# Clamping seven experts' weights to ternary values on GpSimd instead of VectorE, in a fused block of attention and quantised experts

## The chip, the cores and the metric

The kernel runs on one core of one Trainium2 chip. The metric is device microseconds for one execution, lower is better. The core has five engines that run their own instruction streams and wait for each other by semaphores: TensorE (PE in the profile), VectorE (DVE), ScalarE (ACT), GpSimd (POOL) and SyncE (SP), which here only issues loads and stores.

## The reference, cut to what matters

Four layers follow one another on `x` of 16 x 64 x 256 values: a cross attention with 32 heads of width 8, a mixture of eight experts with ternary weights, a latent cross attention, and a mixture of 32 masked experts. The change touches the weights of the second layer:

```python
def weight_quant(w):
    scale = 1.0 / jnp.maximum(jnp.mean(jnp.abs(w)), EPS)
    return jnp.clip(jnp.round(w * scale), -1.0, 1.0) / scale

def expert_ffn(x, gw, uw, dw):          # for each of the 8 experts
    gate = bitlinear(x, gw)
    up = bitlinear(x, uw)
    activated = up * jnp.square(jax.nn.relu(gate))
    return bitlinear(activated, dw)
```

Each of the 24 matrices (gate, up and down of eight experts) is divided by its own mean magnitude, rounded, and clipped to -1, 0 or 1.

## The kernel before, in words

The 1024 tokens are eight tiles of 128 rows. The first layer goes tile by tile, and the weights of one expert are quantised beside each tile, so that tile `t` and expert `t` share one turn of the loops on TensorE, ScalarE and VectorE. Nothing orders the work but the program order of each engine and its semaphores.

One turn of the first layer runs so. TensorE makes the scores of a tile (`natural`, L650) and VectorE takes the row maxima of each head straight from four PSUM banks (`maxima`, L1426). VectorE splits the maxima into three bfloat16 parts (`split_max`, L1433 to L1436), TensorE turns them (L660), VectorE copies them out (`unturn_max`, L1442), and TensorE subtracts them from the scores (`less_max`, L674). ScalarE takes the exponentials (L1166), TensorE turns the probabilities (L683), ScalarE copies them out (L1172), TensorE weighs the values (`weigh`, L698), ScalarE copies the result (L1188), TensorE turns it back (L705), and VectorE divides and adds to `X` (`add_att`, L1447 to L1451). The scores of tile `t + 1` (L650) wait for all four exponentials of tile `t`.

The weights pass through four hands. SyncE loads expert `e` into one of three buffers `raw` (it waits for `raw_used`). ScalarE sums the magnitudes of the three matrices (`magnitudes`, L1180, which uses `W` as a place to write to), TensorE adds over the rows (L667), and VectorE takes mean and reciprocal (`mean`, L1456 to L1458). VectorE then scales the three matrices, takes the minimum with 1 and rounds them to 16-bit whole numbers that lie in the place of the bfloat16 weights (`over_mean`, L1461, three instructions of 128 x 1024 values, the last of which adds one to `raw_used`). Last, one instruction of 128 x 3072 values clamps these whole numbers to -1..1 and writes bfloat16 into the same place (`ternary_of`, L1464).

The order on VectorE in turn `t` is: `mean(t)`, `over_mean(t, 0)`, the maxima of tile `t + 1` and their split, `add_att(t - 1)`, `over_mean` of the two other matrices, a wait for `raw_used` (VectorE's own count), `ternary_of(t)`, `queries(t + 3)` (L1421, the normalised rows `qn`, up to turn 4), and `statistics` (L1398). Turn 6 also centres the router's weights (`r_raw`, L1504 to L1506).

GpSimd has little to do in this layer. It builds constants, waits for the context and the tables, and rotates the keys of the third layer: four `tensor_tensor` on 128 x 1024 or 128 x 512 values for `kvr2` and four of half that size for `kvr` (L559 to L562, each waiting for the one before), one copy (L563), and three instructions on 23 columns (L564 to L566). It then waits for `roots_ready`, which VectorE gives at the end of the layer, and normalises four tiles of `XN` (L568, L570). TensorE needs the rotated keys after the router's logits (L721, L767).

At the end of the layer TensorE weighs the values of the last tile (L698, after VectorE's `att` of the tile before, L1448), turns the result, and computes the router's logits (L721) and the turned keys (L767). ScalarE copies them out, and VectorE picks the two best experts of each token (L458, L461). The first matmul with the ternary weights comes after that.

Of the kernel before, what the change touches and what calls it, by code (L numbers as in the profile page):

```python
# [7 lines left out]
F32, F32R, BF16, I16, I32, U32 = mybir.dt.float32, mybir.dt.float32r, mybir.dt.bfloat16, mybir.dt.int16, mybir.dt.int32, mybir.dt.uint32  # L8
ALU, ACT, AX = mybir.AluOpType, mybir.ActivationFunctionType, mybir.AxisListType
P = 128  # L10
NT = 8
# [9 lines left out]
NE = 8  # L21
# [75 lines left out]
def build(nc, x, ctx_in, cst_in, sel_in, kv_in, router_w, ffn_w, fold_in,  # L97
          weight_t, scale, masks_t, router_dt, out):
    with ExitStack() as ctx:
# [3 lines left out]
        def sb(name, shape, dt=F32):  # L103
            n = int(np.prod(shape[1:])) * (2 if dt == BF16 else 4)
            at = place[0]
            place[0] = (at + n + 31) // 32 * 32
            places[name] = at
            return nc.alloc_sbuf_tensor_at(name, shape, dt, offset=at)
# [5 lines left out]
        def sem(name):  # L114
            return ctx.enter_context(nc.semaphore(name))
# [38 lines left out]
        W = sb("W", [P, NE, 3, 4 * H], BF16)  # L154
# [179 lines left out]
        raw_used, w_summed, w_total, w_rec_ready, hid_acted = (sem(n) for n in ("raw_used", "w_summed", "w_total", "w_rec_ready", "hid_acted"))  # L334
# [204 lines left out]
        def _(pool):  # L539
# [9 lines left out]
            link(pool.memset(before[:], 0.0))  # L549
            pool.affine_select(out=before[:], in_=before[:], compare_op=ALU.is_ge, fill=1.0, base=0,  # L550
                               pattern=[[-1, P]], channel_multiplier=1).then_inc(bconsts_built, 1)
            pool.wait_ge(ctx_loaded, 16)
            pool.wait_ge(cst_loaded, 16)
            for dst, src in ((kvr2[:], ctx2), (kvr[:, :, 0, :], ctxn)):
                n = src.shape[1]
                r = rot[:, 0:n, :]
                cos = cst[:, None, C_KCOS:C_KCOS + S].to_broadcast([P, n, S])
                sin = cst[:, None, C_KSIN:C_KSIN + S].to_broadcast([P, n, S])
                link(pool.tensor_tensor(dst, src, cos, ALU.mult))  # L559
                link(pool.tensor_tensor(r[:, :, 0:32], src[:, :, 32:64], sin[:, :, 0:32], ALU.mult))  # L560
                link(pool.tensor_tensor(r[:, :, 32:64], src[:, :, 0:32], sin[:, :, 32:64], ALU.mult))
                link(pool.tensor_tensor(dst, dst, r, ALU.add))  # L562
            pool.tensor_copy(kvr[:, :, 1, :], kvr[:, :, 0, :]).then_inc(kv_rotated, 1)  # L563
            link(pool.tensor_scalar(spare[:], cst[:, C_IOTA:C_IOTA + NBLK], float(P), float(2 * NT * P), ALU.mult, ALU.add))  # L564
            link(pool.tensor_scalar(slot_of[:, 0, :], spare[:], -1.0, None, ALU.mult))
            pool.tensor_scalar(slot_of[:, 1, :], spare[:], -1.0, float(NT * P), ALU.mult, ALU.add).then_inc(bconsts_built, 1)  # L566
            pool.wait_ge(roots_ready, 1)
            link(pool.tensor_scalar(less_mean[:], mv[:, :, 0], -1.0, 0.0, ALU.mult, ALU.add))  # L568
            for t in range(NT // 2, NT):
# [820 lines left out]
        def _(dve):  # L1390
# [5 lines left out]
            def statistics(tiles):  # L1396
                for t in tiles:
                    ins = dve.bn_stats(stats[:, t, :], X[:, t, :])  # L1398
                link(ins)
# [18 lines left out]
            def queries(t):  # L1418
                if t >= 2:
                    dve.wait_ge(q_turned, t - 1)  # L1420
                dve.tensor_scalar(qn[t % 2][:], X[:, t, :], mv[:, t, 0:1], rstd_q[:, t:t + 1], ALU.subtract,  # L1421
                                  ALU.mult).then_inc(qn_ready, 1)

            def maxima(t, kvl):
                dve.wait_ge(nat_ready, 4 * t + kvl + 1)
                dve.tensor_reduce(mx[:, kvl, :], bank[kvl][:].rearrange("p (h s) -> p h s", s=S), AX.X, ALU.max).then_inc(nat_read, 1)  # L1426

            def split_max(t):
                dve.wait_ge(nat_read, 4 * t + 4)
                if t:  # L1430
                    dve.wait_ge(mx_turned, t)
                m = mx[:].rearrange("p a h -> p (a h)")
                link(dve.tensor_copy(mx_parts[:, 0, :], m))  # L1433
                link(dve.tensor_tensor(mx_rest[:], m, mx_parts[:, 0, :], ALU.subtract))
                link(dve.tensor_copy(mx_parts[:, 1, :], mx_rest[:]))
                dve.tensor_tensor(mx_parts[:, 2, :], mx_rest[:], mx_parts[:, 1, :], ALU.subtract).then_inc(mx_ready, 1)  # L1436

            def unturn_max(t):
                dve.wait_ge(mx_turned, t + 1)
                if t >= 2:  # L1440
                    dve.wait_ge(scores_ready, 4 * t - 4)
                dve.tensor_copy(mxT[t % 2][:], bank[7].bitcast(BF16)[0:96, 4 * P:5 * P]).then_inc(mxT_ready, 1)  # L1442

            def add_att(t):
                dve.wait_ge(o_turned, t + 1)
                o = bank[6][:].rearrange("p (n a) -> p n a", a=32)[:, :, 0:2 * (HD + 1)].rearrange("p n (g e) -> p n g e", g=2)
                link(dve.reciprocal(den_rec[:], o[:, :, :, HD]))  # L1447
                dve.tensor_tensor(att[:].rearrange("p (n g d) -> p n g d", g=2, d=HD), o[:, :, :, 0:HD],  # L1448
                                  den_rec[:, :, :, None].to_broadcast([P, NPAIR, 2, HD]), ALU.mult).then_inc(att_read, 1)
                dve.wait_ge(att_read, t + 1)  # L1450
                dve.tensor_tensor(X[:, t, :], X[:, t, :], att[:], ALU.add).then_inc(x1_ready, 1)  # L1451

            def mean(e):

                dve.wait_ge(w_total, e + 1)
                link(dve.tensor_scalar(w_sum2[:], bank[7][:, 3 * P:3 * P + 3], 1.0 / (FF * H), EPS, ALU.mult, ALU.max))  # L1456
                dve.tensor_copy(w_mean[:, e, :], w_sum2[:])
                dve.reciprocal(w_rec[e % 2][:], w_sum2[:]).then_inc(w_rec_ready, 1)  # L1458

            def over_mean(e, m):  # L1460
                return dve.tensor_scalar(W[:, e, m, :].bitcast(I16), raw[e % 3][:, m, :], w_rec[e % 2][:, m:m + 1], 1.0, ALU.mult, ALU.min)  # L1461

            def ternary_of(e):
                dve.tensor_scalar(W[:, e], W[:, e].bitcast(I16), 1.0, -1.0, ALU.min, ALU.max)  # L1464
# [17 lines left out]
            for t in range(NT):  # L1482
                mean(t)
                dve.wait_ge(w_rec_ready, t + 1)
                over_mean(t, 0)
                if t + 1 < NT:
                    for kvl in range(4):
                        maxima(t + 1, kvl)
                    split_max(t + 1)
                    unturn_max(t + 1)  # L1490
                if t:
                    add_att(t - 1)
                over_mean(t, 1)
                over_mean(t, 2).then_inc(raw_used, 1)
                dve.wait_ge(raw_used, t + 1)
                ternary_of(t)
                if t + 3 < NT:
                    queries(t + 3)
                if t:
                    dve.wait_ge(x1_ready, t)  # L1500
                    statistics([t - 1])
                if t == NT - 2:
                    dve.wait_ge(r_loaded, 16)
                    link(dve.bn_stats(r_stats[:], r_raw[:]))  # L1504
                    link(dve.bn_aggr(r_mv[:], r_stats[:]))
                    dve.tensor_scalar(r_raw[:], r_raw[:], r_mv[:, 0:1], None, ALU.subtract).then_inc(r_centred, 1)  # L1506
# [275 lines left out]
            n = 8 * NGROUP  # L1782
# [162 lines left out]
```

## Time and profile before

| | us |
|---|---|
| median of 3 runs | 478.03 |
| lowest and highest | 476.23 and 480.19 |
| the profiled execution's own time | 480.91 |
| its span in the trace | 479.0 |
| VectorE busy in the span | 347.0 (72%) |
| GpSimd busy in the span | 137.9 (29%) |
| ScalarE busy in the span | 213.7 (45%) |

A span is the time from the first to the last instruction of the profiled execution. In the rows below the first number of a timeline's row is the start in us from the span's start and the second the duration in us; what stands in square brackets is how long the engine was idle before, and what released it. In the chain of waits the rows are the pieces that ended last, in order of time.

### The profile page before, as it was taken

The numbers are of one execution on the slowest core, as the hardware profiler recorded it, in microseconds if no ns is written. First come the engines' busy times: TensorE is split into PE (matmuls) and PEld (weight loads), VectorE is DVE, ScalarE is ACT, GpSimd is POOL, SyncE is SP. The second block draws the span as 40 slices with busy tenths as digits, with TensorE's granted clock in tenths as the row PEclk, the third lists the DMA queues.
The fourth block names the chain that finished last, engine by engine and source line by source line (L and its number), as shares of the span: only waits on it lengthen the run. The fifth ranks groups of instructions, "written<-read, shape, count | busy, mean of one in ns | idle before, by whom it ended". The sixth has DMA issues, their size and how long they took to land.

```text
span 479.0 us, 10598 instructions
## 1 busy us (share of the span) xinstructions
PE 379.1 (79%) x3676; PEld 259.6 (54%) x3677; DVE 347.0 (72%) x876; ACT 213.7 (45%) x474; POOL 137.9 (29%) x147
## 2 busy tenths in 40 slices
PE   2566867771687778797989999999999989548991
PEld 1344545671244444575555664664655878436881
DVE  4998898979788989386686876977868525663551
ACT  1578787825278778479010231221211321224440
POOL 1064000020667774300031421412403410161332
PEclk9989798955589999899999999999999999859997
DMA  8975562041144661171021120220220201341010
GB/s 299 423 300 189 191 219 104 10 168 46 39 132 152 196 200 57 46 263 36 1 90 47 42 90 9 82 89 2 89 89 1 89 1 54 124 130 58 25 35 22
DMA packets 16895, 50.77 MB, mean 106 GB/s; under 512 B 2072, under 2 KB 6304, under 8 KB 14800
## 3 DMA queue, kind: packets, MB, share of 16 engines
q1 hardware_dynamic: 13984, 42.46, 24.6%
q0 software_dynamic: 2864, 7.68, 5.3%
q8 instruction: 30, 0.49, 0.4%
q14 instruction: 17, 0.14, 0.1%
HBM read 43.44 MB, written 6.69 MB: 105 GB/s over the span
## 4 chain that ended last, share of the span: by engine, by line
PE 61%; DVE 14%; ACT 10%; issue 8%; POOL 5%; DMA 1%; ACTq 0%; DVEq 0%; POOLq 0%
PE bank L941 15%; PE bank L1147 7%; PE bank L953 6%; PE bank L1024 6%; PE bank L964 3%; PE bank L837 3%; PE bank L650 2%; PE bank L1000 2%; PE bank L977 2%; DVE mx L1426 2%; PE bank L803 2%; POOL y_rows L589 2%; ACT pnat L1166 2%; ACT W L1180 2%; POOL xg L582 1%
## 5 line engine op out<-in xcount | busy, mean ns | idle before, releaser
L1637 DVE TENSOR_TENSOR roped<-bank,cst 128x512 f32<-128x512 f32 x96 | 61.8, 686 | 30.2 <-PE bank L941 28.6
L596 POOL TENSOR_TENSOR WE<-WE,wT 128x512 f32<-128x512 f32 x32 | 40.5, 1299 | 140.9 <-DMA WE<-_L_ffn_expert_masks_dram 140.9
L1307 ACT ACTIVATE qrT<-bank 128x512 f32<-128x512 f32 x16 | 8.7, 596 | 82.2 <-PE bank L964 82.2
L941 PE MATMUL bank<-XNT_hi,AW_hi 128*128 128x512 f32 x96 | 41.3, 430 | 2.3 <-DVE roped L1637 1.6
L941 PE MATMUL bank<-XNT_hi,AW_lo 128*128 128x512 f32 x96 | 37.8, 394 | 0.0
L941 PE MATMUL bank<-XNT_lo,AW_hi 128*128 128x512 f32 x96 | 37.8, 393 | 0.0
L953 PE MATMUL bank<-roped,MW 128*64 128x512 f32 x128 | 31.0, 605 | 0.0
L1024 PE MATMUL bank<-VW,ctxT 128*128 128x256 f32 x128 | 30.8, 386 | 0.0
L941 PEld LDWEIGHTS bank<-XNT_hi,AW_hi 128*128 128x128 f32 x96 | 18.0, 187 | 22.0 <-DVE roped L1637 12.1
L582 POOL DMA_INDIRECT xg<-x_rows,owner_b x23 | 22.8, 993 | 24.0 <-DVE owner_b L420 14.8
L803 PE MATMUL bank<-W,xgT 128*128 x92 | 27.1, 422 | 2.2 <-ACT xgT L1243 2.2
L589 POOL DMA_INDIRECT y_rows<-y,slot x23 | 22.7, 986 | 17.8 <-ACT y L1261 14.4
L1172 ACT ACTIVATE pT<-bank 128x512 f32<-128x512 f32 x32 | 19.3, 604 | 15.9 <-PE bank L683 15.9
L1180 ACT ACTIVATE W<-raw 128x1024 bf16<-128x1024 f32 x24 | 25.4, 1061 | 0.0
L1024 PEld LDWEIGHTS bank<-VW,ctxT 128*128 128x128 f32 x128 | 23.2, 190 | 3.5 <-issue 0.8
L814 PE MATMUL bank<-identf,hid 128*128 128x128 f32 x92 | 15.5, 292 | 11.7 <-ACT hid L1265 6.9
L1426 DVE TENSOR_REDUCE mx<-bank 128x8 f32<-128x512 f32 x32 | 19.8, 681 | 5.1 <-PE bank L650 5.1
L1147 PE MATMUL bank<-WE,pT_d 128*128 x80 | 21.5, 409 | 1.5 <-ACT pT_d L1385 1.3
L1255 ACT ACTIVATE hidT<-bank,less_magic 128x512 bf16<-128x512 f32 x23 | 15.8, 687 | 12.3 <-PE bank L814 11.6
L683 PE MATMUL bank<-identf,pnat 128*128 128x128 f32 x128 | 20.8, 298 | 0.0
L941 PEld LDWEIGHTS bank<-XNT_hi,AW_lo 128*128 128x128 f32 x96 | 18.0, 188 | 4.3
L1301 ACT ACTIVATE prob<-prob 128x512 f32<-128x512 f32 x16 | 10.1, 632 | 22.3 <-DVE prob L1647 22.3
(297 smaller groups left out, 893.9 us busy)
## 6 DMA issues: line engine op xcount, KB each, us to landing
raw<-in_L_ffn_w_dram SPq DMA_DIRECT2D x8, 1536.0 KB, 6.4
fold<-in_L_xattn_fold_dram SPq DMA_DIRECT2D x8, 1024.0 KB, 5.2
WE<-_L_ffn_expert_masks_dram SPq DMA_DIRECT2D x8, 1024.0 KB, 5.4
kv<-in_keys_values_dram SPq DMA_DIRECT2D x8, 656.0 KB, 7.6
yg<-y_rows SPq DMA_DIRECT2D x8, 256.0 KB, 4.7
x_tok<-pay SPq DMA_DIRECT2D x8, 256.0 KB, 2.3
X<-in_x_dram SPq DMA_DIRECT2D x4, 256.0 KB, 9.3
ctx_sb<-in_ctx_dram SPq DMA_DIRECT2D x1, 768.0 KB, 18.4
```

The costliest lines, as they stand in the source:

```text
L582: pool.indirect_dma_start(out=xg[j % 4][:].bitcast(U32), out_offset=None, in_=x_rows, in_offset=bass.IndirectOffsetOnAxis(ap=RB.owner[:, j ...
L589: pool.indirect_dma_start(out=y_rows, out_offset=bass.IndirectOffsetOnAxis(ap=slot[:, b:b + 1], axis=0), in_=y[b % 4][:], in_offset=None). ...
L596: pool.tensor_tensor(WE[:, e], WE[:, e], wT[:], ALU.mult).then_inc(WE_ready, 1)
L683: mm = pe.transpose(bank[4 + kvl % 2][:, c * P:(c + 1) * P], pnat[kvl][:, c * P:(c + 1) * P], identf[:])
L803: mm = pe.matmul(bank[2 + 2 * m - par][:], xgT[par][:, k * P:(k + 1) * P], W[:, bass.ds(e, 1), m, k * FF:(k + 1) * FF].rearrange("p a i -> ...
L941: mm = pe.matmul(bank[g][:], a[:, k, c * P:(c + 1) * P], b[:, k, g * 512:(g + 1) * 512], start=k == 0 and i == 0, stop=k == 1 and i == 2)
L953: pe.matmul(bank[2 + g][half(h, g) * S:(half(h, g) + 1) * S, :], MW[u][:, r, at:at + S], roped[n][:, r, :], start=r == 0, stop=False, skip ...
L1024: mm = pe.matmul(bank[t % 4][:, 0:H], ctxT[:, u, t * P:(t + 1) * P], VW[:, u, :], start=u == 0, stop=u == NU - 1)
L1147: mm = pe.matmul(bank[4 + r % 4][:, 0:H], pT_d[r % 4][:, k * P:(k + 1) * P], WE_k[:, bass.ds(e, 1), k, :].rearrange("p a o -> p (a o)"), s ...
L1180: ins = act.activation(W[:, e, m, :], raw[e % 3][:, m, :], ACT.Abs, accum_out=w_sum[e % 2][:, m:m + 1])
L1426: dve.tensor_reduce(mx[:, kvl, :], bank[kvl][:].rearrange("p (h s) -> p h s", s=S), AX.X, ALU.max).then_inc(nat_read, 1)
L1637: ins = dve.tensor_tensor(roped[n][:, r, :].rearrange("p (b s) -> p b s", s=S), src, cst[:, None, at:at + S].to_broadcast([P, 8, S]), ALU. ...
```

## The change

GpSimd runs `ternary_of` for experts 0 to 6, between and behind its instructions for the rotation, each after a wait for the expert's `raw_used`. VectorE keeps only expert 7. The instruction is the same in shape, operations and place.

```diff
@@ GpSimd @@
+            def ternary_of(e):
+                pool.wait_ge(raw_used, e + 1)
+                pool.tensor_scalar(W[:, e], W[:, e].bitcast(I16), 1.0, -1.0, ALU.min, ALU.max)
+
+            ternary_of(0)
             pool.wait_ge(ctx_loaded, 16)
             pool.wait_ge(cst_loaded, 16)
             for dst, src in ((kvr2[:], ctx2), (kvr[:, :, 0, :], ctxn)):
...
                 link(pool.tensor_tensor(dst, dst, r, ALU.add))
+                ternary_of(1 if n == 2 * NT else 2)
             pool.tensor_copy(kvr[:, :, 1, :], kvr[:, :, 0, :]).then_inc(kv_rotated, 1)
...
+            for e in range(3, NE - 1):
+                ternary_of(e)
             pool.wait_ge(roots_ready, 1)
@@ VectorE @@
                 over_mean(t, 2).then_inc(raw_used, 1)
                 dve.wait_ge(raw_used, t + 1)
-                ternary_of(t)
+                if t == NT - 1:
+                    ternary_of(t)
                 if t + 3 < NT:
                     queries(t + 3)
```

## Rows read from the trace of the kernel before

**Rows 1.** Busy us (and instructions) of PE, PEld, DVE, ACT and POOL, by stretch

```profile
14.00:46.00 32.00, 20.76 (x303) 14.67 (x303) 29.74 (x76) 22.06 (x44) 13.63 (x12) 0.95 0.74 292
46.00:94.00 48.00, 35.86 (x605) 26.96 (x605) 42.71 (x107) 38.24 (x79) 0.00 (x0) 0.89 0.39 142
```

**Rows 2.** The chain of waits, from 32 to 72 us

```profile
32.26 2.48 DVE mx L1426 x4
...
43.42 2.49 DVE mx L1426 x4
...
65.93 1.04 ACT W L1180 x2
```

**Rows 3.** VectorE in order of time: clamps, and maxima that waited for TensorE

```profile
26.61 0.96 DVE L1464 TENSOR_SCALAR W<-W 128x3072 bf16<-128x3072 int16 x1
...
53.72 2.48 DVE L1426 TENSOR_REDUCE mx<-bank 128x8 f32<-128x512 f32 x4 [0.86 <-PE bank L650]
...
60.20 0.96 DVE L1464 TENSOR_SCALAR W<-W 128x3072 bf16<-128x3072 int16 x1
...
69.48 0.96 DVE L1464 TENSOR_SCALAR W<-W 128x3072 bf16<-128x3072 int16 x1
...
82.09 2.48 DVE L1426 TENSOR_REDUCE mx<-bank 128x8 f32<-128x512 f32 x4 [0.77 <-PE bank L650]
...
88.57 0.96 DVE L1464 TENSOR_SCALAR W<-W 128x3072 bf16<-128x3072 int16 x1
```

**Rows 4.** VectorE in order of time: around the clamp of expert 3

```profile
59.42 0.75 DVE L1461 TENSOR_SCALAR W<-raw,w_rec 128x1024 int16<-128x1024 f32 x1
...
61.08 0.41 DVE L1421 TENSOR_SCALAR qn<-X,mv,rstd_q 128x256 f32<-128x256 f32 x1
...
62.33 0.75 DVE L1461 TENSOR_SCALAR W<-raw,w_rec 128x1024 int16<-128x1024 f32 x1
63.00 2.48 DVE L1426 TENSOR_REDUCE mx<-bank 128x8 f32<-128x512 f32 x4
...
66.71 0.22 DVE L1442 COPY mxT<-bank 96x128 bf16<-96x128 bf16 x1 [0.35 <-PE bank L660]
```

**Rows 5.** VectorE and GpSimd in order of time, during the rotation

```profile
27.17 2.27 POOL L559 TENSOR_TENSOR kvr<-ctx_sb,cst 128x1024 f32<-128x1024 f32 x1 [24.24 <-DMA ctx_sb<-in_ctx_dram]
27.48 2.10 DVE L1421 TENSOR_SCALAR qn<-X,mv,rstd_q 128x256 f32<-128x256 f32 x1
29.51 1.10 POOL L560 TENSOR_TENSOR rot<-ctx_sb,cst 128x512 f32<-128x512 f32 x1
29.69 0.96 DVE L1457 COPY w_mean<-w_sum 128x3 f32<-128x3 f32 x1
30.70 1.09 POOL L561 TENSOR_TENSOR rot<-ctx_sb,cst 128x512 f32<-128x512 f32 x1
30.75 1.58 DVE L1461 TENSOR_SCALAR W<-raw,w_rec 128x1024 int16<-128x1024 f32 x1
```

**Rows 6.** GpSimd: groups by line, shapes apart (busy us, mean ns)

```profile
L577 POOL TENSOR_SCALAR hid<-hid,hs 128x512 f32<-128x512 f32 x12 | 8.4, 700 | 0.5
...
L600 POOL MEMSET acc<- 128x2048 f32 x1 | 1.8, 1807 | 0.1
...
L568 POOL TENSOR_SCALAR less_mean<-mv 128x8 f32<-128x8 f32 x1 | 0.2, 203 | 60.4 <-DVEq L1512 60.4
```

**Rows 7.** VectorE and GpSimd in order of time: both on `XN`

```profile
103.12 0.57 POOL L570 TENSOR_SCALAR XN<-X,less_mean,rstd 128x256 f32<-128x256 f32 x1
...
103.19 0.64 DVE L1514 TENSOR_SCALAR XN<-X,mv,rstd 128x256 f32<-128x256 f32 x1
```

**Rows 8.** The end of the layer: VectorE and TensorE in order of time

```profile
90.56 0.34 DVE L1506 TENSOR_SCALAR r_raw<-r_raw,r_mv 8x256 f32<-8x256 f32 x1
...
92.33 0.42 DVE L1448 TENSOR_TENSOR att<-bank,den_rec 128x256 f32<-128x256 f32 x1
...
95.00 0.64 PE L698 MATMUL bank<-pT,kv 128*18 128x64 f32 x32 [0.33 <-ACT pT L1172]
```

## The prediction

> **What bounds the kernel now.** I read the busy times by stretch first, to see how full VectorE and GpSimd are where the clamp runs. From 14 to 46 us VectorE is busy for 29.74 of 32 us, and from 46 to 94 us for 42.71 of 48, while GpSimd works for 13.63 us in the first stretch and not at all in the second [rows 1]. So GpSimd has the time. The chain of waits, read second, says what the clamp is worth. In its pieces from about 15 to 47 us nearly everything is VectorE (the maxima at 32.26 and 43.42 us belong to it), but from there to 95 us it is a loop of ScalarE and TensorE, with ScalarE's sums of the weights in it (65.93 us) [rows 2]. A turn of that loop is 69.48 - 60.20 = 9.28 us [rows 3]. VectorE's own turn is hardly shorter: the wait of 0.35 us for the turned maxima is its only one in such a turn [rows 4], so it works for about 8.9 us. Taking work from VectorE can therefore pay in the first two turns only, and putting more than some 0.4 us of stall on it makes it the bound again, up to what the next engine can wait.
>
> Third I read VectorE and GpSimd side by side, because GpSimd is to run while VectorE goes on. During the rotation some VectorE instructions stretch to the end of the GpSimd instruction beside them. `qn`, 0.41 us elsewhere [rows 4], starts at 27.48 and ends at 29.58, behind a GpSimd instruction that ends at 29.44; the copy of three columns takes 0.96 us and ends at 30.65, with GpSimd's instruction at 30.61; a scaling that takes 0.75 us elsewhere ends at 32.33, 0.54 us after GpSimd's at 31.79 [rows 5]. So these forms (copy and `tensor_scalar` from SBUF to SBUF) stand still while GpSimd runs. GpSimd's `tensor_scalar` does this as well as its `tensor_tensor`: VectorE's `XN` at 103.19 us takes 0.64 us and ends 0.14 after GpSimd's at 103.69 [rows 7]. The maxima, read from PSUM, kept their 2.48 us beside GpSimd (32.26 us) [rows 2].
>
> **The change part by part.** *Removed:* seven clamps of 0.96 us on VectorE; the next instruction starts 0.88 us after each (60.20 to 61.08) [rows 3, 4].
>
> *Added:* seven clamps on GpSimd of length D. The trace has no GpSimd instruction of 3072 values or on 16-bit whole numbers, so D is bounded by its neighbours [rows 6]. `tensor_scalar` takes 0.203 us for 8 columns and 0.700 us for 512: a line through both gives 0.986 ns a column and D = 0.203 + 3064 x 0.000986 = 3.2 us. Six times the 512-column time gives 4.2 us, an upper end. From below, the largest memset needs 1.807/2048 = 0.88 ns a column, 2.7 us, and if more of the 0.700 us is a fixed cost than 0.2, D comes down: a line through the 0.57 us for 256 columns of `XN` [rows 7] and the 0.700 us gives 2.0 us. I take 3.2 us, because its two rows are the same operation with little beside them, and keep 2.2 (2.0 runs faster than the memset writes) and 4.2.
>
> The Trainium skill (GPSIMD Engine Reference, Engine selection) sends elementwise work to VectorE and calls GpSimd roughly line-rate with one input; an estimate from its 1.2 GHz and the 0.2 us start is 2.8 us, by which the sum below would be about +4.5 us. The same page (Elementwise — side-by-side cycle accounting) gives 1.8 cycles an element for a tight loop, an estimate of 4.6 us and about +17 us; the trace's 0.700 us for 512 columns lies between the two.
>
> *The new wait.* GpSimd is released by `raw_used`, at the moment VectorE used to start the clamp; call that S. VectorE goes on to `qn` (S to S + 0.4). VectorE's clamp used to start 0.03 us after the scaling that it waits for (59.42 + 0.75 to 60.20) [rows 3, 4], and no row shows GpSimd quicker than that, so I let `qn` through first. The clamp then runs from S + 0.4 to S + 3.6. The copy of the three means stands behind it, ends 0.04 us later, and the scaling of the next expert's first matrix starts 0.10 us after that, at S + 3.74. The maxima follow 0.67 us later, as at 62.33 to 63.00, at S + 4.41. They came at S + 2.80 (63.00 - 60.20). So a full turn loses 1.61 us, and its length is 9.28 + 1.61 = 10.9 us. Behind the late maxima wait TensorE's subtraction, ScalarE's exponentials, and all of the loop; their slack of about 1.3 us (ScalarE starts an exponential that much after the scores could be ready) holds one such stall, not a repeated one, since VectorE is then busy or blocked all the time.
>
> The turns one by one, delay of S in brackets:
> - Turn 0: after the clamp GpSimd starts the rotation's first instruction (2.27 us [rows 5]), which catches the scaling: 3.67 + 2.27 + 0.54 - 0.07 = 6.41 us after S to the maxima, 5.65 before (32.26 - 26.61), +0.76. The rotation, itself 3.1 us later, then holds the first cast of the maxima's split some 0.9 us more, but is over before three later instructions that it stretched in the old order (a second cast, the addition to `X`, a scaling: 0.33 + 0.39 + 0.35 us). [+0.65 at S1]
> - Turn 1: the second rotation's first instruction, 1.09 us, does the same: 3.67 + 1.09 + 0.54 - 0.07 = 5.23, 2.80 before, +2.4. [+3.05]
> - Turn 2: the copy for `kvr` (a 512-column instruction, 0.7 us) catches the scaling and adds 0.4; of the 1.61 the 0.86 us that the maxima waited for TensorE anyway come off [rows 3]: +1.1. [+4.15]
> - Turns 3 and 4: +1.6 each. [+7.35]
> - Turn 5: there is no `qn`, before or after; 1.61 less the wait of 0.77 us for TensorE [rows 3], +0.8. [+8.15]
> - Turn 6: GpSimd starts at S + 0.1. The centring of the router's weights (8 rows) is of the form that stands still; it ends 0.14 after the clamp, at S + 3.44, where it ended at 90.90 - 88.57 = 2.33 [rows 3, 8], +1.1. [+9.25]
>
> At the end VectorE's `att`, due at 92.75, comes at 102.0. TensorE's weighing of the last tile, 1.1 us, waits for it and ends at 103.1; it ended at 95.64, held by ScalarE's copy [rows 8]. So 1.8 us of the delay vanish there and +7.5 us remain; VectorE's own way to the router's choice, where it kept the clamp of expert 7, is +8.1 us with 0.8 us of idle in front of its join. GpSimd has ended its last clamp several us before `roots_ready`, so `XN` is not later for it, and the loads, which wait for `raw_used`, move with the turns. Everything behind the layer moves by the same +7.5 us.
>
> The sum: 480.91 + 7.5 = 488.4 us against the profiled execution. That execution was 2.9 us above the median of the runs, so I put the same difference on the median: 478.0 + 7.5 = 485.5 us. Each us of D counts seven times.
>
> **The rivals.**
> - *D is short, about 2.2 us.* For: 256 columns take nearly as long as 512 [rows 6, 7]. Against: the memset's rate [rows 6]. A turn of 7.65 + D = 9.85 us is still a little over 9.28, and 7.5 - 7 x 1.0 = +0.5: 478.5 us.
> - *GpSimd is slow on this form, 4.2 us.* 7.5 + 7 x 1.0 = +14.5: 492.5 us. For: whole numbers in and bfloat16 out, which no row shows. Against: in-place form and few operations.
> - *GpSimd gets ahead of `qn`.* Then `qn`, the statistics and the sums come behind the clamp instead of beside it: the maxima at S + 0.1 + D + 1.75, 0.64 us later in each of five turns, +3.2: 488.7 us. For: both are released by the same instruction. Against: VectorE's 0.03 us above.
> - *Not slower: the clamp doesn't hold VectorE back (a 16-bit form that blocks nothing, or runs in under about 1.6 us).* Place: the copy of the three means after each clamp. It decides at 7.65 + D = 9.28, D = 1.63 us, below which ScalarE's loop is the bound again. The gain is then the two clamps on VectorE's stretch of the chain, 2 x 0.88 = 1.8 us: 476.2 us. The other five gain nothing, for the loop there is ScalarE's and TensorE's. Against: [rows 7], a GpSimd `tensor_scalar` that did hold VectorE. The Trainium skill (SBUF — State Buffer, Who interferes with whom) says too that whoever issues first has the shared ports for the whole instruction.
>
> **How the numbers follow.** The forecast (D about 2.8 to 3.7 us) 0.46; slow clamp 0.13; GpSimd ahead of `qn` 0.10; short clamp 0.22; not slower 0.09. About 1% (4.8 us) is what a measurement of this kernel tells from no change. Slower by over 1% takes D over 2.8 us: most of the first three cases, 0.67. Within 1%: the short clamp, most of the last, a little of the first, 0.29. Faster by over 1%, -4.8 us, would need most of 7 x 0.88 = 6.2 us on the path, which the chain speaks against: 0.04. The range runs from the short clamp's side, 477.5, to a slow clamp, 493.5; the forecast's own, for D from 2.8 to 3.7, is 482.5 to 489.
>
> **What would show it right or wrong.** Right: GpSimd's seven clamps of about 3.2 us, one a turn; on VectorE the copy of the three means at about 2.7 us instead of 0.17 in turns 3 to 5; turns of about 10.9 us between the `qn`; the pieces of the chain in the first layer VectorE's and GpSimd's in place of ScalarE's; the second layer's start some 7.5 us later, and from there on the same length. Wrong in size: clamps of another length, with the same picture. Wrong in kind: means of 0.17 us beside a running clamp (no block), turns of 9.3 us in spite of blocked means (more slack than I count), or a `qn` of 3 us (the other order).

## The result: slower by 1.3%, and the profile after

The changed kernel takes 488.23 us (median of 6 runs, 482.00 to 489.81) against 478.45 us before (6 runs, 476.12 to 480.19). The ratio is 1.0134, 95% interval 1.0085 to 1.0182, which on 478.45 us is +6.4 us (+4.1 to +8.7). A second set of six runs gave 1.0142 (1.0087 to 1.0197). Executions of one kernel differ by several us with the clock that TensorE is granted; the ratio compares like with like and the bare medians don't, so 9.8 us between the medians is not the price of the change.

The profiled execution has its own time at 489.74 us and a span of 487.8 us, 8.8 us more than before. The page's parts 1, 4 and 5 (busy time; the shares of the chain of work that ended last, in which DVE had 14% and ACT 10% before; and the new group):

```profile
PE 382.1 (78%) x3670; PEld 263.5 (54%) x3677; DVE 354.9 (73%) x869; ACT 215.5 (44%) x474; POOL 156.6 (32%) x154
...
PE 59%; DVE 20%; issue 9%; ACT 5%; POOL 5%; DMA 1%; DVEq 0%; ACTq 0%; POOLq 0%
...
L554 POOL TENSOR_SCALAR W<-W 128x3072 bf16<-128x3072 int16 x7 | 19.5, 2788 | 61.2 <-DVE W L1469 61.2
```

One line is the point of the case: VectorE is busy for 354.9 us, 7.9 us more than before, although seven clamps of 0.96 us left it. Work went away and busy time grew, so instructions that stayed got longer; in a profile, an instruction that stands still counts as busy. The clamp on GpSimd takes 2.79 us on average.

VectorE in order of time, in turn 1 (the first five rows), in turn 3 (from 60.57 us) and at the start of turn 4's `qn`. It answers to [rows 4]; L1421 is now L1429, L1461 is L1469, L1426 is L1434, L1457 is L1465:

```profile
40.48 0.41 DVE L1429 TENSOR_SCALAR qn<-X,mv,rstd_q 128x256 f32<-128x256 f32 x1
40.81 0.42 DVE L1406 BATCH_NORM_STATS2 stats<-X 128x6 f32<-128x256 f32 x1
41.26 0.16 DVE L1464 TENSOR_SCALAR w_sum<-bank 128x3 f32<-128x3 f32 x1
41.46 2.06 DVE L1465 COPY w_mean<-w_sum 128x3 f32<-128x3 f32 x1
...
45.03 2.47 DVE L1434 TENSOR_REDUCE mx<-bank 128x8 f32<-128x512 f32 x4
...
60.57 1.41 DVE L1469 TENSOR_SCALAR W<-raw,w_rec 128x1024 int16<-128x1024 f32 x2
62.01 2.94 DVE L1429 TENSOR_SCALAR qn<-X,mv,rstd_q 128x256 f32<-128x256 f32 x1
...
65.52 0.17 DVE L1465 COPY w_mean<-w_sum 128x3 f32<-128x3 f32 x1
...
66.47 2.48 DVE L1434 TENSOR_REDUCE mx<-bank 128x8 f32<-128x512 f32 x4
...
72.95 2.94 DVE L1429 TENSOR_SCALAR qn<-X,mv,rstd_q 128x256 f32<-128x256 f32 x1
```

GpSimd in the same turns:

```profile
40.60 2.89 POOL L554 TENSOR_SCALAR W<-W 128x3072 bf16<-128x3072 int16 x1 [3.95 <-DVE W L1469]
...
62.06 2.75 POOL L554 TENSOR_SCALAR W<-W 128x3072 bf16<-128x3072 int16 x1 [5.63 <-DVE W L1469]
73.00 2.75 POOL L554 TENSOR_SCALAR W<-W 128x3072 bf16<-128x3072 int16 x1 [8.19 <-DVE W L1469]
```

Read the ends together. In turn 1 the copy of three columns (0.17 us before) ends at 43.52, 0.03 us after the clamp. The two instructions before it run in the middle of the clamp and are not held: the statistics, which read `X` in SBUF (0.42 us), and a `tensor_scalar` that reads its sums from PSUM (0.16 us), as long as in the kernel before. In turn 3 it is `qn` (0.41 us elsewhere) that ends at 64.95, 0.14 us after the clamp. Between the two `qn` of turns 3 and 4 lie 72.95 - 62.01 = 10.94 us, where a turn took 9.28 [rows 3]. The chain of waits says the same. From 57 to 87 us, where before it was ScalarE's and TensorE's loop [rows 2], it is now VectorE's (a few of its pieces; "issue" is here the stretch inside the blocked `qn`):

```profile
60.57 1.42 DVE W L1469 x2
62.05 2.83 issue
64.88 0.42 DVE stats L1406
...
66.47 2.49 DVE mx L1434 x4
...
71.50 1.42 DVE W L1469 x2
72.98 2.83 issue
...
84.54 2.16 DVE w_mean L1465
```

How the delay grows: S, the start of what follows the last scaling on VectorE, came before at 26.61, 40.62, 49.98, 60.20, 69.48, 78.76, 88.57 us and the last clamp at 94.58. After, the same places are 26.72, 40.48, 51.50, 62.01, 72.95, 83.88, 94.04 and 100.66. The delay is +0.1, -0.1, +1.5, +1.8, +3.5, +5.1, +5.5, +6.1. The router's choice (L458) starts at 113.62 us instead of 107.70, +5.9.

The other 2.9 us of the 8.8 lie behind the layer, in code that nobody touched. More than half of it is in one place: eight matmuls of the last layer (L1024 before, L1032 after) that took 1.97 us at a granted clock of 1.00 take 3.63 us at 0.53. Whether the change did that is a question for the second trace of the kernel before, below.

### The profile page after: what moved, and what is told of

The parts are those of the page before. It is cut to its first block, busy times and chain, and to the rows that moved or that the text cites. A ratio compares the mean times of both kernels' runs of the same rounds, so it can differ in the third digit from the quotient of the medians.

```text
span 487.8 us, 10601 instructions
## 1 busy us (share of the span) xinstructions
PE 382.1 (78%) x3670; PEld 263.5 (54%) x3677; DVE 354.9 (73%) x869; ACT 215.5 (44%) x474; POOL 156.6 (32%) x154
## 4 chain that ended last, share of the span: by engine, by line
PE 59%; DVE 20%; issue 9%; ACT 5%; POOL 5%; DMA 1%; DVEq 0%; ACTq 0%; POOLq 0%
PE bank L949 14%; PE bank L1155 7%; PE bank L1032 6%; PE bank L961 6%; DVE mx L1434 4%; PE bank L972 3%; PE bank L845 3%; PE bank L1008 2%; PE bank L985 2%; POOL y_rows L597 2%; PE bank L811 2%; DVE w_mean L1465 2%; DVE W L1469 2%; POOL xg L590 1%; PE bank L874 1%
## 5 line engine op out<-in xcount | busy, mean ns | idle before, releaser
L554 POOL TENSOR_SCALAR W<-W 128x3072 bf16<-128x3072 int16 x7 | 19.5, 2788 | 61.2 <-DVE W L1469 61.2
L1032 PE MATMUL bank<-VW,ctxT 128*128 128x256 f32 x128 | 32.5, 401 | 0.0
L811 PE MATMUL bank<-W,xgT 128*128 x86 | 25.6, 423 | 2.9 <-ACT xgT L1251 2.6
L1032 PEld LDWEIGHTS bank<-VW,ctxT 128*128 128x128 f32 x128 | 24.2, 198 | 3.8 <-issue 0.8
L1434 DVE TENSOR_REDUCE mx<-bank 128x8 f32<-128x512 f32 x32 | 19.8, 681 | 3.5 <-PE bank L658 3.5
```

Of the source, the lines that this page charges most:

```text
L811: mm = pe.matmul(bank[2 + 2 * m - par][:], xgT[par][:, k * P:(k + 1) * P], W[:, bass.ds(e, 1), m, k * FF:(k + 1) * FF].rearrange("p a i -> ...
L1032: mm = pe.matmul(bank[t % 4][:, 0:H], ctxT[:, u, t * P:(t + 1) * P], VW[:, u, :], start=u == 0, stop=u == NU - 1)
```

## The experiments

The theory: GpSimd's clamp holds VectorE's copy and `tensor_scalar` instructions still for as long as it runs, and seven such holds make the loss. The rivals: the lost time is the order of GpSimd and `qn`; the wait or the hand-over of `W` costs it, not the hold; or the clamps on VectorE were worth more than I thought, in either direction. The start of the router's choice is quoted for each trace as the end of the first layer.

**1. The same clamps at a harmless moment (`window`).** The clamp of expert e starts only when VectorE has scaled the first matrix of the next expert, so that it runs beside the maxima, which are read from PSUM.

```diff
                 pool.wait_ge(raw_used, e + 1)
+                pool.wait_ge(first_scaled, e + 2)
                 pool.tensor_scalar(W[:, e], W[:, e].bitcast(I16), 1.0, -1.0, ALU.min, ALU.max)
...
-                over_mean(t, 0)
+                over_mean(t, 0).then_inc(first_scaled, 1)
```

> GpSimd keeps its seven clamps, but each also waits until VectorE has scaled the first matrix of the next expert, so that it runs beside the maxima, which VectorE reads from PSUM. If the loss is VectorE standing still behind a running clamp (copy and tensor_scalar forms only), the 2.75 us of a clamp fall on 2.48 us of maxima and little is left: turns of about 9.3 us again, 476 to 479 us, at or just under before. If the loss is anything else in having the clamp on GpSimd (later weights, a busy GpSimd, the order of its queue), it stays near 485 us or above, since each clamp now comes later.

Measured: 480.41 us, ratio to the kernel before 1.0004 (0.9962 to 1.0045); the router's choice at 106.25 us. VectorE and GpSimd in turn 3:

```profile
60.20 0.41 DVE L1430 TENSOR_SCALAR qn<-X,mv,rstd_q 128x256 f32<-128x256 f32 x1
...
61.18 0.17 DVE L1466 COPY w_mean<-w_sum 128x3 f32<-128x3 f32 x1
...
62.37 2.75 POOL L555 TENSOR_SCALAR W<-W 128x3072 bf16<-128x3072 int16 x1 [4.70 <-DVE W L1470]
62.54 2.48 DVE L1435 TENSOR_REDUCE mx<-bank 128x8 f32<-128x512 f32 x4 [0.33 <-PE bank L659]
```

The clamp is as long as in the changed kernel and runs on the same engine, with one wait more. It covers the maxima (62.54 to 65.02) and they keep their 2.48 us; the copy has its 0.17 us back. The whole loss is gone (the ratio allows 0.5% either way). So it was neither GpSimd's speed as such nor the hand-over, but what VectorE had to do at that moment.

**2. The clamp in three pieces (`split`).** VectorE can slip in between pieces.

```diff
-                pool.tensor_scalar(W[:, e], W[:, e].bitcast(I16), 1.0, -1.0, ALU.min, ALU.max)
+                for m in range(3):
+                    pool.tensor_scalar(W[:, e, m], W[:, e, m].bitcast(I16), 1.0, -1.0, ALU.min, ALU.max)
```

> Each clamp on GpSimd is cut into three instructions of 128x1024, at the same place. If GpSimd holds VectorE back for one instruction at a time, an instruction of VectorE waits for the rest of one piece of about 1 us, not for 2.75 us: qn, the copy of the means and the scaling go in between, and a turn loses 0 to 0.3 us in place of 1.6: 478 to 480 us. If what counts is GpSimd's total time beside VectorE, it stays at 485 us.

Measured: 481.58 us, ratio 1.0054 (1.0021 to 1.0087), above the 478 to 480 us that I expected; the router's choice at 109.43 us. VectorE and GpSimd in turn 3:

```profile
61.08 1.23 DVE L1430 TENSOR_SCALAR qn<-X,mv,rstd_q 128x256 f32<-128x256 f32 x1
61.12 3.08 POOL L555 TENSOR_SCALAR W<-W 128x1024 bf16<-128x1024 int16 x3 [4.04 <-DVE W L1470]
...
62.87 0.35 DVE L1466 COPY w_mean<-w_sum 128x3 f32<-128x3 f32 x1
...
63.33 1.42 DVE L1470 TENSOR_SCALAR W<-raw,w_rec 128x1024 int16<-128x1024 f32 x1
```

The three pieces take longer together than the one (3.08 us against 2.75), and yet more than half of the loss is gone: `qn` waits 0.82 us for the first piece, the copy 0.18 for the second, the scaling 0.67 for the third, 1.67 us in all where the changed kernel's `qn` alone lost 2.53. VectorE gets its turn at each end of a GpSimd instruction. The hold is per instruction, and its price is at most what is left of that instruction. What I had too low is the loss in a turn: the `qn` of turns 3 and 4 lie 71.31 - 61.08 = 10.23 us apart, about 0.95 more than before and not 0 to 0.3, since three instructions of such a turn wait.

**3. `qn` always first (`qn_first`).** The clamps of experts 0 to 4 also wait until `qn` is done, which takes the rival order away.

```diff
                 pool.wait_ge(raw_used, e + 1)
+                if e + 3 < NE:
+                    pool.wait_ge(qn_ready, e + 4)
```

> The clamps of experts 0 to 4 on GpSimd also wait for VectorE's qn of that turn, so that qn always comes first. If it costs something that GpSimd got ahead of qn in turns 0, 3 and 4, these turns get 0.5 to 0.6 us shorter each and the time falls by 1.5 to 2 us against the changed kernel: about 483 us. If the order doesn't matter, because the copy of the means stands behind the clamp in any case, it stays at 485 us.

Measured: 487.34 us, ratio 1.0158 (1.0114 to 1.0201); the router's choice at 114.13 us, no earlier than in the changed kernel. In turn 3 `qn` has its 0.41 us again, and the copy takes over the stall:

```profile
63.14 0.41 DVE L1431 TENSOR_SCALAR qn<-X,mv,rstd_q 128x256 f32<-128x256 f32 x1
...
63.71 2.75 POOL L556 TENSOR_SCALAR W<-W 128x3072 bf16<-128x3072 int16 x1 [6.15 <-DVE qn L1431]
...
64.12 2.36 DVE L1467 COPY w_mean<-w_sum 128x3 f32<-128x3 f32 x1
...
67.25 2.48 DVE L1436 TENSOR_REDUCE mx<-bank 128x8 f32<-128x512 f32 x4
```

From the start of `qn` to the maxima it is 67.25 - 63.14 = 4.11 us here, against 4.46 (66.47 - 62.01) in the changed kernel, where GpSimd was first: 0.35 us better in turns 3 and 4. But a clamp that waits for `qn` starts 0.57 us behind its start (63.71), where without that wait it began 0.12 us behind it (40.60, turn 1). So turns 1 and 2, in which `qn` had been first already, lose about as much as turns 3 and 4 gain. This way of forcing the order is worth nothing; what the order itself is worth can be read from `scratch`, in the next experiment.

**4. The hold without the hand-over (`scratch`), and no clamps at all (`no_clamp`).** In `no_clamp` VectorE clamps only expert 7; experts 0 to 6 get their scaled weights as bfloat16, neither rounded nor limited from below. In `scratch` GpSimd in addition runs seven clamps of the same form at the same moments, on a tile that nobody reads; the weights are as in `no_clamp`.

```diff
@@ both, VectorE @@
-                return dve.tensor_scalar(W[:, e, m, :].bitcast(I16), raw...
+                into = W[:, e, m, :].bitcast(I16) if e == NE - 1 else W[:, e, m, :]
+                return dve.tensor_scalar(into, raw...
...
-                ternary_of(t)
+                if t == NT - 1:
+                    ternary_of(t)
@@ scratch, GpSimd @@
+            def ternary_of(e):
+                pool.wait_ge(raw_used, e + 1)
+                link(pool.tensor_scalar(scratch[:], scratch[:].bitcast(I16), 1.0, -1.0, ALU.min, ALU.max))
```

> Nobody clamps experts 0 to 6: VectorE writes their scaled weights as bfloat16, not rounded and with no lower limit, and GpSimd has nothing added. This is what the removal alone is worth. If ScalarE and TensorE bound the later turns, only the two clamps in VectorE's stretch of the chain count: 476 to 477.5 us, -1 to -2 against before. If VectorE bounds every turn, all seven count: 472 us.

> As the run without clamps (VectorE writes experts 0 to 6 as bfloat16, unrounded and without a lower limit), but GpSimd runs seven clamps of the same form, length and release on a scratch tile that nobody reads. If the loss is only that VectorE stands still while GpSimd runs, nothing else of the clamp matters and the first layer ends where it ends in the changed kernel: the router's choice at 113 to 114 us, 484 to 487 us in all. If the loss came through the weights (who writes them, and when), the choice stays near the 103.4 us of the run without clamps and the time near 476 us.

Measured: `no_clamp` 477.54 us, ratio 0.9921 (0.9877 to 0.9966), the router's choice at 103.39 us; `scratch` 484.60 us, ratio 1.0122 (1.0070 to 1.0173), the router's choice at 111.71 us. In `scratch`, turns 3 and 4:

```profile
62.59 2.94 DVE L1432 TENSOR_SCALAR qn<-X,mv,rstd_q 128x256 f32<-128x256 f32 x1
62.64 2.75 POOL L557 TENSOR_SCALAR scratch<-scratch 128x3072 bf16<-128x3072 int16 x1 [5.63 <-DVE W L1473]
...
67.04 2.48 DVE L1437 TENSOR_REDUCE mx<-bank 128x8 f32<-128x512 f32 x4
...
73.51 0.41 DVE L1432 TENSOR_SCALAR qn<-X,mv,rstd_q 128x256 f32<-128x256 f32 x1
73.63 2.90 POOL L557 TENSOR_SCALAR scratch<-scratch 128x3072 bf16<-128x3072 int16 x1 [8.25 <-DVE W L1473]
...
74.49 2.06 DVE L1468 COPY w_mean<-w_sum 128x3 f32<-128x3 f32 x1
...
77.33 2.48 DVE L1437 TENSOR_REDUCE mx<-bank 128x8 f32<-128x512 f32 x4
```

GpSimd's instructions touch nothing that VectorE, TensorE or ScalarE uses, no engine waits for them, and the picture and the loss are those of the change: 1.0122 beside 1.0134 and 1.0142. The hold alone is the cause; this is shown. The two turns also give the price of the order, since GpSimd is first in one and `qn` in the other: from `qn` to the maxima it is 67.04 - 62.59 = 4.45 us and 77.33 - 73.51 = 3.82 us, 0.63 us a turn. The gain of `no_clamp`, -4.3 us at the router's choice, was a miss: 1.8 us was forecast.

**5. Why 4.3 and not 1.8: both kernels traced again (`before_again`, `no_clamp_again`).** The first trace of before had a granted clock of 0.66 from 46 to 56 us and that of `no_clamp` 1.00.

> The kernel before once more, for a second trace of it. In the first trace the router's choice began at 107.7 us, with a granted clock of 0.66 from 46 to 56 us, and leaving out the seven clamps (no_clamp) brought it to 103.4 us, with a granted clock of 1.00 there. Theory A (part of the 4.3 us is TensorE's clock in that one execution, and the clamps themselves are worth about 1.8 us): the choice begins at about 105.5 us in an execution whose clock stays up from 46 to 56 us. Theory B (the clamps cost 4.3 us or bring the clock down by themselves): it begins at 107 to 108 us again, with a low clock at 46 to 56 us. Ratio to before 1.00 within 0.5% under both.

> no_clamp once more, for a second trace. Theory A: the router's choice may lie anywhere from 103.4 to about 106 us, later where the clock falls in the turns. Theory B: 103 to 104 us again. Ratio about 0.992.

Measured: the kernel before again at a ratio of 0.9976 to itself (0.9937 to 1.0016), the router's choice at 107.79 us; `no_clamp` again 0.9987 (0.9950 to 1.0025), at 106.26 us. The stretches 26 to 46, 46 to 56, 56 to 80 and 80 to 92 us, first of the kernel before again, then of the second `no_clamp` (the columns are those of [rows 1]; the granted clock is the third number from the end):

```profile
26.00:46.00 20.00, 12.64 (x244) 9.31 (x241) 19.18 (x33) 15.40 (x31) 13.83 (x12) 0.91 0.58 216
46.00:56.00 10.00, 6.17 (x125) 4.72 (x125) 9.19 (x25) 8.60 (x20) 0.00 (x0) 1.00 0.66 256
56.00:80.00 24.00, 19.77 (x325) 14.71 (x325) 21.70 (x54) 19.32 (x40) 0.00 (x0) 0.79 0.48 177
80.00:92.00 12.00, 9.38 (x137) 7.20 (x138) 9.90 (x26) 8.79 (x18) 0.00 (x0) 0.86 0.01 2
```

```profile
26.00:46.00 20.00, 14.08 (x245) 10.45 (x243) 17.52 (x35) 15.32 (x31) 12.94 (x12) 0.83 0.60 224
46.00:56.00 10.00, 7.00 (x131) 5.21 (x132) 8.28 (x22) 8.60 (x19) 0.00 (x0) 1.00 0.72 276
56.00:80.00 24.00, 16.83 (x331) 12.42 (x337) 19.37 (x49) 20.01 (x41) 0.00 (x0) 0.92 0.44 162
80.00:92.00 12.00, 9.55 (x143) 7.34 (x128) 9.26 (x25) 8.24 (x17) 0.00 (x0) 0.87 0.01 2
```

Theory A is half right. For it: the second `no_clamp`, with a clock of 0.83 and 0.87 where the first had 1.00 and 1.00, ends the layer only 1.4 to 1.5 us before either trace of the kernel before: close to the 1.8 us of the prediction, and over 1% in neither set. Against it: the kernel before did not come to 105.5 us with its clock up at 46 to 56 us; the low stretch was now from 56 to 80 us (0.79, where the first trace had 1.00). No trace here has the kernel before with a high clock throughout, so what of the 4.3 us is clamps and what clock stays open; the two ratios with their intervals put the worth of the clamps between nothing and 1.2%.

The same pair answers the question left above. The eight matmuls of the last layer, first in the changed kernel, then in the kernel before traced again:

```profile
396.96 3.63 PE L1032 MATMUL bank<-VW,ctxT 128*128 128x256 f32 x8
```

```profile
391.12 3.59 PE L1024 MATMUL bank<-VW,ctxT 128*128 128x256 f32 x8
```

The kernel before does the same in its longer execution, at a granted clock of 0.53 as well. From the router's choice to the end of the span the traces take 371.3 and 374.2 us (before), 374.2 and 373.7 (changed), 370.2 (`window`), 370.0 (`split`), 368.7 (`qn_first`), 371.0 (`scratch`), 372.9 and 368.4 (`no_clamp`): some 6 us of scatter in untouched code, without order. So nothing here charges the 2.9 us to the change, and the ratio, +6.4 us (4.1 to 8.7), is close to the 5.9 of the layer.

**6. The other user of the same window: the rotation (`rot_beside_maxima`, `rot_again`).** In the kernel before, GpSimd's rotation holds VectorE in the same way [rows 5]. Here all clamps stay on VectorE, and the rotation's instructions wait for `first_scaled`, so that they run beside the maxima of tiles 2 to 6.

```diff
+                turn = 0 if n == 2 * NT else 3
+                pool.wait_ge(first_scaled, turn + 2)
                 link(pool.tensor_tensor(dst, src, cos, ALU.mult))
+                if n == 2 * NT:
+                    pool.wait_ge(first_scaled, turn + 3)
...
+                pool.wait_ge(first_scaled, turn + (4 if n == 2 * NT else 3))
                 link(pool.tensor_tensor(dst, dst, r, ALU.add))
```

> The kernel before, with all eight clamps on VectorE, but GpSimd's rotation of the keys is held so that its pieces run beside the maxima of tiles 2 to 6. If GpSimd's old rotation already held VectorE back (2.1, 0.96, 1.58 and 1.01 us for instructions of 0.41, 0.17, 0.75 and 0.18 us, on the chain that ends last), the maxima of tile 3 come 1.5 to 3 us sooner than 43.4 us, and the time falls by 1.5 to 4 us against before: 474 to 477 us. If these stalls were covered by ScalarE's loop, it stays at 478 us.

> rot_beside_maxima once more. If the rotation held VectorE in the kernel before, the router's choice begins at about 103 us again and the ratio is 0.985 to 0.995; if the first time was an execution with a good clock, the choice begins at 105 to 107 us and the ratio is 1.00.

Measured: the first time a ratio of 0.9893 (0.9815 to 0.9972) and the router's choice at 102.94 us, the second time 0.9991 (0.9949 to 1.0033) and 108.48 us. The first looked like a version that beats both kernels, but its ratio rests on three executions of 474 to 475 us; the second, on more, takes that back. VectorE and the chain of waits in the second:

```profile
29.49 0.75 DVE L1466 TENSOR_SCALAR W<-raw,w_rec 128x1024 int16<-128x1024 f32 x1
33.16 2.48 DVE L1431 TENSOR_REDUCE mx<-bank 128x8 f32<-128x512 f32 x4 [2.92 <-PE bank L655]
```

```profile
29.01 1.06 ACT pnat L1171 x3
...
31.11 2.02 PE bank L655 x32
```

VectorE's scaling has its 0.75 us (1.58 in [rows 5]), so it is free of the rotation. But then it waits 2.92 us for the scores: the chain has gone to ScalarE's and TensorE's loop, and with a granted clock of 0.79 from 26 to 46 us (1.00 the first time) the 32 matmuls of a tile take 2.02 us (1.12 the first time). In these two traces the clock decides whether VectorE's gain shows.

**7. Two clamps and the rotation beside the maxima (`two_and_rot`).** Experts 0 and 1 are clamped on GpSimd, then comes the rotation with the waits of experiment 6 two turns later (not shown), all beside maxima; VectorE keeps six clamps.

```diff
+            for e in range(2):
                 pool.wait_ge(raw_used, e + 1)
+                pool.wait_ge(first_scaled, e + 2)
                 pool.tensor_scalar(W[:, e], W[:, e].bitcast(I16), 1.0, -1.0, ALU.min, ALU.max)
...
-                if t == NT - 1:
+                if t >= 2:
                     ternary_of(t)
```

> GpSimd takes only the clamps of experts 0 and 1, beside the maxima of tiles 2 and 3, and its rotation follows in pieces beside the maxima of tiles 4 to 7; VectorE keeps the other six clamps. The two clamps were all of them that lay on VectorE's stretch of the chain, and nothing on GpSimd is left that stands in VectorE's way. Theory: at or below the run with the rotation alone held back, and as good as the run without clamps: 473 to 476 us. Rival (VectorE bounds the later turns too): clamps 2 to 6 cost 0.88 us each there and it ends 2 to 4 us above the run without clamps.

Measured: 480.19 us, ratio 1.0025 (0.9986 to 1.0063), the router's choice at 106.44 us. A miss: no gain. Together with the two runs above, no arrangement tried here is repeatably faster than the kernel before.

**8. The changed kernel again (`changed_again`).**

> The changed kernel once more, on the same chip as the others of this call. Every theory: slower than before by 1.2 to 1.7%, 484 to 488 us, with the router's choice at 113 to 114 us.

Measured: 486.63 us, ratio 1.0142 (1.0087 to 1.0197). The maxima of the last tile start at 87.42 us, 87.47 in the first trace, so the turns repeat to 0.05 us up to there; the router's choice is at 111.88 us, not at the expected 113 to 114 (113.62 in the first trace). Behind the last maxima there is only TensorE, ScalarE and VectorE's tail, and the granted clock from 92 to 104 us was 0.89 here, 0.78 in the first trace and 0.74 in the kernel before. By the clock the first trace is therefore the like one to compare with; in this one the layer ends 4.1 to 4.2 us later than in the two traces of before, not 5.9.

## Why the prediction was right

485.5 us was forecast, 478.0 + 7.5; the ratio says +6.4 (4.1 to 8.7).

- *What bounds the kernel* was right. VectorE has no room in a turn, and a stall of a few us in each makes it the bound: the chain changed from ScalarE and TensorE to VectorE.
- *These forms stand still while GpSimd runs* was right and is shown by itself in `scratch`, `window` and `split`. The Trainium skill (SBUF — State Buffer, Who interferes with whom) has the same rule, that the engine which issues first keeps the shared ports for the whole instruction and `tensor_reduce` stays out of it; the trace agrees that the wait lasts to the end of GpSimd's instruction, with 2.19 us added to a copy in one order (2.36 less 0.17, turn 3 of `qn_first`) and 2.53 to `qn` in the other, and that the maxima get none added. Which engine came first can't be read from the recorded starts, as the last section says.
- *The turn of 10.9 us* came out at 10.94, but for partly the wrong reason: D was 2.75 us instead of 3.2, which takes 0.45 off, and GpSimd got ahead of `qn` there, which puts 0.5 back on.
- *D = 3.2 us* is the term that was mis-sized. The two rows that I drew the line through made 0.99 ns a column; the memset's rate that I had set as the lower bound, 0.88 ns [rows 6], was nearer: 2.75 us for 3072 columns is 0.90. The delay of S over the layer was +9.25 in the prediction and is +6.1: 3.1 us less, and seven times 0.45 us is 3.15. So the multiplier of seven held. By turn the forecast was +0.65, 2.4, 1.1, 1.6, 1.6, 0.8, 1.1; measured are -0.25, 1.66, 0.29, 1.66, 1.65, 0.35, 0.61 between the S above. With 0.45 taken off each, what is left differs by -0.45 in turn 0 (there `qn` was held, against the forecast, but the first cast of the maxima's split took 0.99 us, as in the kernel before, and not the 0.9 us more that I had put down), by about -0.3 in turns 1 and 2, where the clamp ran beside `qn` instead of behind it, and by +0.5 in turns 3 and 4, where it came before `qn`. That these cancel is luck. The estimate from the Trainium skill (GPSIMD Engine Reference, Engine selection), 2.8 us, was nearer than mine; the 1.8 cycles an element that I took from the same page (Elementwise — side-by-side cycle accounting), 4.6 us, are not what this instruction takes. That section of the Trainium skill also has 1.03 cycles an element where at most two operations fall on each, as here; an estimate from it is 2.6 us without the start.
- *The join at the end gives 1.8 us back* failed. I had VectorE's delayed `att` run into slack in front of TensorE's last weighing. But the weighing waits for ScalarE's copy, which hangs on the maxima of the last tile, and these were late as well (+5.4 at 87.47 us). VectorE in order of time at `att`, then TensorE's two weighings of the last tile, to be set beside [rows 8]:

```profile
98.41 0.42 DVE L1456 TENSOR_TENSOR att<-bank,den_rec 128x256 f32<-128x256 f32 x1
```

```profile
99.87 0.64 PE L706 MATMUL bank<-pT,kv 128*18 128x64 f32 x32
100.84 0.64 PE L706 MATMUL bank<-pT,kv 128*18 128x64 f32 x32 [0.33 <-ACT pT L1180]
```

  `att` is late by 6.1 us, the last weighing by 5.8: both sides moved together and nothing vanished. The two errors account for the sum: 7.5, less 3.15, plus the 1.6 of the 1.75 us that the join did not give back, is 5.95 us, and the router's choice is 5.92 us later. It is luck that they point opposite ways: with D at 2.75 us and the join as forecast the sum would have given +4.35 us.
- *`qn` goes first*, the choice against the third rival, was wrong in three of the five turns (0, 3 and 4); the `qn` of 3 us that the prediction named as a sign of the other order was there. The order is worth 0.63 us a turn (`scratch`), the rival's 0.64. Against the forecast, turns 3 and 4 cost some 0.5 us more each, but the other three were cheaper by about as much, so the rival's +3.2 us did not come.
- *The removal is worth 1.8 us* stays between the two measurements of `no_clamp`, as said.

Of the rivals, the short clamp (2.2 us) and the slow one (4.2) are refuted by the length itself. "Not slower" named one of the right places, the copy of the means, and the right condition, a clamp that doesn't hold VectorE; `window` makes that condition true by moving the clamp, and lands at no change.

## What to carry to other kernels

- Before you move work to an engine with spare time, list what the engine beside it runs at that moment. In these traces a GpSimd instruction on SBUF holds VectorE's copies and `tensor_scalar` from SBUF to SBUF until it ends; a three-column copy then takes over 2 us. Put GpSimd's long instructions beside VectorE work that it doesn't hold, here the maxima read from PSUM (1.0134 became 1.0004), or cut them into pieces (1.0054).
- Look at busy time with suspicion: an engine that lost 6.7 us of work and shows 7.9 us more is being held.
- A gain of about 1% that rests on one trace or one set of runs is not yet a gain when the clock moves by itself: 0.9893 became 0.9991.

## What the runs showed that I had not expected

- The start in the record doesn't tell which engine is held. In the changed kernel VectorE's `qn` starts at 62.01 and 72.95 us, GpSimd's clamp 0.05 us later each time, and it is `qn` that waits (2.94 us). Where the gap is 0.12 us (40.48 and 40.60) `qn` goes through in 0.41 us and the clamp takes 2.89 instead of 2.75. `scratch` shows both in one trace, at gaps of 0.05 and 0.12 us.
- A piece of 1024 columns of the clamp costs about 1.03 us (3.08 for three), so cutting it adds some 0.3 us in all where VectorE is the one that waits; in turns 1 and 2 of `split`, where VectorE's instructions get in between, the three take 3.63 us.
- TensorE's granted clock can change the picture of a stretch as much as the edit does. The same stretch, 46 to 56 us, was granted 0.66 and 1.00 in two executions of the kernel before, and the layer ended at the same time in both (107.70 and 107.79 us); in the other the low stretch came from 56 to 80 us (0.79 against 1.00).
